# Quantised activations of a transformer block turned as the low 16-bit halves of their words

## The reference

```
def _act_quant(x):                     # x: tokens x 512, after a layer norm (or the attention's output)
    scale = 127.0 / clip(max(abs(x), axis=-1), 1e-05, None)
    q = clip(round(x * scale), -128, 127) / scale
def _bitlinear(x, w): return _act_quant(x) @ _weight_quant(w).T     # weights are -1, 0, 1 times a scale
q, k, v = bitlinear(x, w_q), bitlinear(x, w_k), bitlinear(x, w_v)
attn = softmax(q k^T / sqrt(32)) v ;   return bitlinear(attn, w_o)
```

## Time and profile before

| | |
|---|---|
| time, median of 3 runs | 1529.88 us (1525.74 to 1530.67) |
| the profiled execution's own time | 1529.94 us |
| its span | 1527.6 us |
| PE, PEld, DVE, ACT, POOL busy | 90%, 75%, 76%, 56%, 26% of the span |
| granted TensorE clock, mean | 0.968 |

### The profile page before, as it was taken

The page is one execution under the profiler, slowest core; times in us unless marked ns, Lnnn a source line. Parts: engine busy times, 40 slices in busy tenths (PEclk is TensorE's granted clock), DMA queues, the critical chain, the costliest instruction groups (busy, mean ns, idle before and its releaser), DMA issues.

```text
span 1527.6 us, 37167 instructions
## 1 busy us (share of the span) xinstructions
PE 1382.0 (90%) x14168; PEld 1142.3 (75%) x14168; DVE 1166.5 (76%) x2255; ACT 861.5 (56%) x1473; POOL 398.7 (26%) x494
## 2 busy tenths in 40 slices
PE   4556657999999998699999999999999999999997
PEld 1221125777777776599999998989899898999996
DVE  4699966888988887577646877778778777677776
ACT  4667734777777776323324656666666666433331
POOL 6600045444445320103211111111111110034333
PEclk8899978999999999799999999999999999999999
DMA  9999952322322211121113677787777776544365
GB/s 345 387 357 352 384 125 76 84 64 63 82 62 71 61 42 57 69 100 56 41 42 124 205 272 244 263 275 242 256 262 248 253 251 229 196 129 150 124 234 179
DMA packets 77904, 269.40 MB, mean 176 GB/s; under 512 B 9696, under 2 KB 10336, under 8 KB 71392
## 3 DMA queue, kind: packets, MB, share of 16 engines
q1 hardware_dynamic: 61360, 223.88, 41.0%
q0 software_dynamic: 16432, 44.05, 11.2%
HBM read 224.12 MB, written 43.78 MB: 175 GB/s over the span
## 4 chain that ended last, share of the span: by engine, by line
PE 32%; DVE 10%; issue 8%; ACT 7%; DMA 2%; ACTq 0%; SPq 0%; POOL 0%; POOLq 0%; DVEq 0%
PE up_ps L1708 6%; PE up_ps L1710 6%; PE up_ps L1709 6%; PE down_ps L1709 4%; PE down_ps L1710 4%; PE down_ps L1708 3%; ACT w_split L1398 3%; DVE w_split L1483 3%; DVE xT_lo L1474 2%; DMA slot_rows<-y_rows 1%; PE up_ps L1742 1%; DVE h L1619 1%; PE up_ps L1737 1%; DVE w_split L1484 1%; ACT h_hi L1420 1%
## 5 line engine op out<-in xcount | busy, mean ns | idle before, releaser
L1708 PE MATMUL up_ps<-xT_hi,w_split 128*128 128x256 f32 x1280 | 366.5, 286 | 15.3 <-DVE xT_lo L1474 8.3
L1710 PE MATMUL up_ps<-xT_hi,w_split 128*128 128x256 f32 x1280 | 362.8, 283 | 0.0
L1709 PE MATMUL up_ps<-xT_lo,w_split 128*128 128x256 f32 x1280 | 362.8, 283 | 0.0
L1708 PEld LDWEIGHTS up_ps<-xT_hi,w_split 128*128 128x128 f32 x1280 | 245.7, 192 | 18.2 <-DVE xT_lo L1474 8.4
L1709 PEld LDWEIGHTS up_ps<-xT_lo,w_split 128*128 128x128 f32 x1280 | 245.9, 192 | 1.3
L1710 PEld LDWEIGHTS up_ps<-xT_hi,w_split 128*128 128x128 f32 x1280 | 245.7, 192 | 0.0
L1420 ACT ACTIVATE h_hi<-h 128x256 fp32r<-128x256 f32 (+1 forms) x192 | 80.2, 418 | 265.4 <-DVE h L1619 203.9
L1371 POOL DMA_INDIRECT xr<-x_rows,slot_tokens x71 | 71.9, 1013 | 425.4 <-PE xT_ps L1803 380.9
L1398 ACT ACTIVATE w_split<-w_stage 128x1408 fp32r<-128x1408 f32 (+1 forms) x123 | 169.3, 1411 | 5.1 <-PE down_ps L1710 1.8
L387 PE MATMUL cross_ps<-W,a_all 128*16 128x512 f32 x500 | 108.6, 658 | 59.8 <-DMA W<-table 59.5
L284 DVE TENSOR_TENSOR acc<-acc,W 128x2560 f32<-128x2560 f32 x46 | 129.7, 2820 | 40.5 <-ACT W L225 37.5
(11 more groups left out here) (295 smaller groups left out, 3004.2 us busy)
## 6 DMA issues: line engine op xcount, KB each, us to landing
W<-table SPq DMA_DIRECT2D x48, 1280.0 KB
w_stage<-packed SPq DMA_DIRECT2D x80, 704.0 KB
w_stage<-packed SPq DMA_DIRECT2D x40, 768.0 KB, 5.2
xr<-x_turned SPq DMA_DIRECT2D x32, 512.0 KB
slot_rows<-y_rows SPq DMA_DIRECT2D x32, 512.0 KB
x_rows<-x SPq DMA_DIRECT2D x32, 256.0 KB, 2.0
x_turned<-x2T SPq DMA_DIRECT2D x32, 256.0 KB, 3.7
out<-H SPq DMA_DIRECT2D x32, 256.0 KB
```

Source lines behind the costliest of these rows:

```text
L1708: pe.matmul(out, a_hi, b_hi, start=first, stop=False)
L1709: pe.matmul(out, a_hi, b_lo, start=False, stop=False)
L1710: return pe.matmul(out, a_lo, b_hi, start=False, stop=last)
```

## The change

Both quantised tiles get 2 to the 14th on top of ROUNDER. The lowest 16 bits of each word then are 16384 + q, which as a 16-bit integer is small and positive, and as a bfloat16 pattern is an ordinary number. PE turns only these halves, seen as a bfloat16 tile with a step of two, against a bfloat16 identity that the kernel already has (`ident_b`), into the first half of `bank[3]`. ACT reads the result as 16-bit integers and takes 16384 off. No instruction is added, removed or put elsewhere on any engine; the turns of `outT`, `x2` and the sums stay in float32.

```
+LOW_HALF = 2.0**14
...
+        turned_words = bank[3][:, :].bitcast(mybir.dt.int16)[:, 0:D].rearrange("p (k t) -> p k t", k=KT)
...
-  act.activation(z2[:, :], attn[:, :], ACT.Copy, bias=ROUNDER, scale=quant2[:, 0:1]).then_inc(z2_done, 1)
+  act.activation(z2[:, :], attn[:, :], ACT.Copy, bias=ROUNDER + LOW_HALF, scale=quant2[:, 0:1]).then_inc(z2_done, 1)
...
-  act.activation(aqT[:, :, :], bank[3][:, :].rearrange("p (k t) -> p k t", k=KT), ACT.Copy, bias=-ROUNDER).then_inc(aqT_done, 1)
+  act.activation(aqT[:, :, :], turned_words, ACT.Copy, bias=-LOW_HALF).then_inc(aqT_done, 1)
...            (z at L698 and xqT at L710 in the same way)
+            def turn_words(tile):
+                words = tile[:, :].bitcast(BF16)[:, 0::2]
+                for k in range(KT):
+                    mm = pe.transpose(bank[3][:, :].bitcast(BF16)[:, k * T:(k + 1) * T], words[:, k * P:(k + 1) * P], ident_b[:, :])
+                return mm
...
-                    turn(bank[3], z[ahead1.b]).then_inc(xq_turned, 1)
+                    turn_words(z[ahead1.b]).then_inc(xq_turned, 1)
...
-                    turn(bank[3], z2).then_inc(aq_turned, 1)
+                    turn_words(z2).then_inc(aq_turned, 1)
```

More of the change, by code:

```diff
@@ L697, in body @@
                     after(act, xq_turned, ahead2.i - 1)
-                    act.activation(z[ahead2.b][:, :], y[ahead2.b][:, :], ACT.Copy, bias=ROUNDER, scale=quant[ahead2.b][:, 0:1]).then_inc(z_done, 1)
+                    act.activation(z[ahead2.b][:, :], y[ahead2.b][:, :], ACT.Copy, bias=ROUNDER + LOW_HALF, scale=quant[ahead2.b][:, 0:1]).then_inc(z_done, 1)
                 if now.yes:
@@ L709, in body @@
                     act.wait_ge(xq_turned, ahead2.next)
-                    act.activation(xqT[ahead2.b][:, :, :], bank[3][:, :].rearrange("p (k t) -> p k t", k=KT), ACT.Copy, bias=-ROUNDER).then_inc(xqT_done, 1)
+                    act.activation(xqT[ahead2.b][:, :, :], turned_words, ACT.Copy, bias=-LOW_HALF).then_inc(xqT_done, 1)
                 if back1.yes:
```

## The result

The change makes the kernel faster: 1523.26 us (median of 19 runs, 1521.3 to 1525.63) against 1528.78 us (19 runs), a ratio of 0.9965 with a 95% interval of 0.9959 to 0.9972, so 4.3 to 6.3 us less. The forecast was 5.4 us less, stated as 1524.5 us from a base of 1529.9; the base is now 1528.78, so the gains are what to compare. One of the runs of before, at 4581 us, is left out of the ratio. The profiled execution has a span of 1523.0 us.

The account below looks back on a forecast made before the run. A step was taken as a closed 11.30 us ring, PE bounding only some pieces and elsewhere waiting for x2, xqT and maxT; 29 x 0.14 = 4.1 plus 1.3 at the ends gave 5.4 us, so 1524.5 us, range 1519 to 1531.5.

Parts of the forecast that it names:

- The turn: PE's four-block turns of z and z2: 0.39 us instead of 0.60 with 16-bit halves.
- Rival A: At PE's turns: a 16-bit turn takes as long as a float32 one, nothing moves, 1530 us; chance 0.22.
- xqT and v: Between x2's turn and v: xqT starts without ACT idling, v comes 0.14 us earlier, then PE's L910 bounds.
- z2 gives nothing: Turn of z2 before L991: PE only waits 0.21 us longer for maxT, so 0 gained per step.
- rival C: Whole steady step: PE really bounds and both turns count in full, 0.42 us a step, 1516.5 us; chance 0.09.
- The copies: ACT's copies xqT and aqT, reading 16-bit integers: 0.60 us as before, 0.81 as upper bound.
- rival B: At ACT's copies: the integer read is slow, at twice 0.60 us giving 1546 us; chance 0.07.
- The steady sum: Steady attention steps from 260 to 591.3 us: 29 steps of 0.14 us, 4.1 us gained.
- The ends of the stage: Attention's first and last turns and one filling step: 0.45 + 0.21 + 0.45 + 0.2, together 1.3 us gained.
- the third sequence: One step while the attention pipeline fills, without x2 ahead: 0.2 us gained.
- the last turn: Far end of attention, where ACT waits 0.78 us for it: 0.45 us gained, as at the start.
- The 0.21 for the step before it: Far end of attention, no k filling PE: of L1014's 0.35 us wait for aqT, 0.21 goes.

Follow-up runs that it names:

- doubled turn of z: Changed kernel with the turn of z issued twice in a row, the same extra PE work between outT's turn and x2's: ratio 0.9990 to the kernel before.
- two doubled turns: Changed kernel with one turn issued twice in a row, z2's in one run, z's in the other: ratios 0.9967 and 0.9990 to the kernel before.
- filling of the kernel before: Kernel before, float32 turns kept, with ACT's e_logit before maxT and a quarter of k's projection before L991: ratio 0.9998 to the kernel before.
- integer read alone: Kernel before with float32 turns kept, but 16384 added and ACT reading every second 16-bit half of the bank as integers: ratio 0.9998.
- only z: Changed kernel with z2's turn put back to float32, so just z is turned by 16-bit halves: 4.1 us faster than the kernel before, ratio 0.9973.
- two quarters of k: Changed kernel with ACT's e_logit before maxT and two of four quarters of k's projection moved before L991: ratio 0.9930 to the kernel before.

## Why the prediction was right

Point by point, in its own order:

- *The turn.* 0.60 to 0.39 us, forecast 0.39; one block lasts 219 ns. The nearest row, the bfloat16 product that reads every second half, held in both properties. Rival A is refuted. By the figure of the Trainium skill, "TensorE: Matmul & The Clock Gate", section "Part 4: PE-mode transpose", the block would have lasted about 275 ns; the measurement decides, and it says 219.
- *xqT and v.* Forecast: v 0.14 us earlier behind the turn of x2, for PE is in L910 until then. Measured 0.15 (0.86 to 0.71). The doubled turn of z gave it all back, which shows that this is the way.
- *z2 gives nothing.* Measured 0.01 us a step, alone and together with z. With the two doubled turns this refutes rival C: equal work on PE is worth 0.01 us in one place and 0.15 in the other. The sum was right, one reason only half: the prediction let PE be free at 431.05 and wait for maxT. The filling of the kernel before showed that L991 comes 0.10 behind the last slot in any case, so the two ways tied. Either way a shorter turn cannot pull L991 forward, because maxT stands behind it.
- *The copies.* 0.60 us, as taken; the integer read alone changed nothing, so rival B is refuted.
- *The steady sum.* 29 steps of 0.14 were forecast as 4.1 us; 29 x 0.15 = 4.4 came.
- *The ends of the stage.* Forecast 1.3 us; the terms add up to 1.7 in the profiles, and lean on the clock. At the start v follows the first turn of z after 235.94 - 234.58 = 1.36 us instead of 1.86, 0.50 for 0.45. In the third sequence v follows the turn of z after 256.69 - 255.53 = 1.16 us instead of 256.21 - 254.83 = 1.38, 0.22 for 0.2. At the far end the last turn gave more than forecast, 0.72 us for 0.45: before, it ran at a granted clock of 0.50, the lower level (four blocks in 1.12 us), and after at 1.00 (0.40 us).

```profile
609.22 1.12 PE L846 MATMUL bank<-ident,z 128*128 128x128 f32 x4 [0.22 <-ACT z L674]
...
611.03 1.89 PE L1014 MATMUL bank<-wT_o,aqT 128*128 128x512 bf16 x4 [0.69 <-ACT aqT L685]
```

```profile
603.85 0.40 PE L858 MATMUL bank<-ident_b,z 128*128 128x128 bf16 x4 [0.22 <-ACT z L679]
604.94 1.89 PE L1026 MATMUL bank<-wT_o,aqT 128*128 128x512 bf16 x4 [0.69 <-ACT aqT L690]
```

The first fence is the kernel before, the second the changed one. In both the output projection behind the turn ran at 0.50. So the clock had fallen before the turn in the first and fell behind it in the second. What sets that moment no run shows, and I would not count on all of the 0.72 us: in the profile of "z twice" the same short turn of z2 ran at 0.50 there (607.01) and took 0.61 us, so at equal clock the change gives 1.12 - 0.61 = 0.51, and the other 0.21 is the clock's. The 0.21 for the step before it was forecast from the wait of L1014 for aqT; L1026 waits the same 0.35 still, since L1003, which stands before it on PE, moved with the turn. From the turn of the maxima to the output projection it went from 1.70 to 1.44 us all the same, 0.26 for 0.21.

How close 5.4 came to 5.5 is in part luck. The terms as measured, 4.4 + 1.7 = 6.1 us, are above the forecast, and the profiled execution of the changed kernel lost some of it again, early in the stage. The same 32 products, before and changed:

```profile
247.03 1.17 PE L941 MATMUL S<-QT,K_T 32*128 32x128 f32 x32 [0.71 <-DVE max_parts L755]
```

```profile
246.19 2.09 PE L953 MATMUL S<-QT,K_T 32*128 32x128 f32 x32 [0.71 <-DVE max_parts L760]
```

The granted clock was 0.50 there in the changed kernel's execution, and 1.00 in that of before. From v of the second sequence to the turn of the maxima it took 5.26 us instead of 3.75, so 1.5 us were lost. The profile of "only z", with the same start of the stage, has 1.00 there. How many of the 19 runs lost this is not shown.

One more thing helps to read single profiles with care: in that of before, one step lasted 12.56 instead of 11.31 us (DVE waited 1.74 us for scores before 335.00, where it waits 0.27 in other steps), which the changed kernel's profile lacks. So the difference between the two profiled spans, 4.6 us, is not the sum of the terms; attention is 5.8 us shorter from its first turn to its last logits product, of which 1.25 is that one step (the other 4.5 are the terms' 6.1 less the 1.5 lost to the clock, within 0.1), and the experts took about 1.5 us longer in that execution. The medians of 19 runs are what the 5.5 us stand on.

## What to carry to other kernels

A busy share of 99% says neither that an engine bounds nor where. Take one step of the pipeline, follow it around from a start to the same start one step later, and ask at each piece whether the engine was free or its input late; a saving counts only in the pieces where it was the engine, or where it feeds the late input. A saving that ends in a wait is not lost: it is a hole of known size, and here moving work from behind the wait into it gave more (0.21 us a step) than the change itself (0.15). Where a wait and an engine's own end lie within 0.1 us of each other, treat them as tied until a run has moved one of them.

## What the runs showed of the hardware

- A transposing matmul of a 128 x 128 block whose stationary operand is every second 16-bit half, read as bfloat16, takes 219 ns and a slot of (0.39 - 0.22) / 3 = 0.057 us, at a granted clock of 1.00. The plain bfloat16 products of k, whose operand has no step, have the same 0.057. In float32 a transposing block takes 273 ns and a slot of 0.11 us.
- ACT reads 512 int16 elements from PSUM in 0.597 us, at a step of one (changed) or two ("integer read"), the same 0.597 as for float32.
- With k's products before them and maxT ready for 0.28 us, the 32-row products of L1004 start 0.09 us behind the last slot of the 128-row stream (429.40 behind 429.31), where equal products follow each other at 0.057. With two quarters of k it is 0.08 (432.40 behind 431.86 + 8 x 0.057 = 432.32). In the kernel before the distance is 0.10 (431.15 behind 431.05), but maxT came only 0.06 before, so that row doesn't show it alone.
- The granted clock of one stretch of the same code differed between executions: 0.50 in the products of 246.19 us of the changed kernel's profile, 1.00 in those of 247.03 before.
